# Opening of a fused conditioning, recurrence and FFN kernel: loads and first products in another order

## The reference, cut to what matters

```python
styles = w @ (affine_w * gain).T + affine_b            # (2, 512), w is 2 x 256
dcoefs = rsqrt(sum((weight * styles)**2, axis=2) + 1e-08)
xm = x * styles[:, None, :]
y = einsum('blc,oc->blo', xm, weight) * dcoefs          # 512 x 512 weight
y = clip(y + bias, -256, 256)

h = rms_norm(y) * norm_w
hs = h @ fc_w.T + fc_b                                  # then fc_r, fc_i, fc_gate:
r, i = sigmoid(h @ fc_r_w.T + ...), sigmoid(h @ fc_i_w.T + ...)
# a gated recurrence over the tokens, an MLP of 1536 columns, then
# a second branch with an int8 product
```

## Time and profile before

| what | value |
|---|---|
| median of the runs | 1724.21 us |
| profiled execution | 1724.23 us |
| its span, first to last instruction | 1722.2 us |
| TensorE busy | 1711.0 us, 99% of the span |
| VectorE, ScalarE, GpSimd busy | 1249.2, 882.0, 728.7 us |

### The profile page before, as it was taken

The page is one execution under the profiler, slowest core; times in us unless marked ns, Lnnn a source line. Parts: engine busy times, 40 slices in busy tenths (PEclk is TensorE's granted clock), DMA queues, the critical chain, the costliest instruction groups (busy, mean ns, idle before and its releaser), DMA issues. The chain is left out here.

```text
span 1722.2 us, 23029 instructions
## 1 busy us (share of the span) xinstructions
PE 1711.0 (99%) x7749; PEld 1385.2 (80%) x7749; DVE 1249.2 (73%) x1842; ACT 882.0 (51%) x1306; POOL 728.7 (42%) x642
## 2 busy tenths in 40 slices
PE   9999999999999999999999999999999999999998
PEld 7888888888888888888888888778787787787776
DVE  7766776658989688687464434447998988888876
ACT  7655556556666576575553222233554444543533
POOL 1122221222677465656571000006656755855823
PEclk9999999999999999999999999999999999999999
DMA  6011101120233434232445666887635444535411
GB/s 211 1 49 50 49 0 49 49 74 25 98 123 105 164 99 147 86 120 89 171 147 191 205 213 212 318 297 257 223 116 156 114 139 146 152 104 163 137 43 61
DMA packets 119959, 221.94 MB, mean 129 GB/s; under 512 B 25442, under 2 KB 25890, under 8 KB 119860
## 3 DMA queue, kind: packets, MB, share of 16 engines
q1 hardware_dynamic: 94308, 161.99, 28.1%
q10 hardware_dynamic: 18384, 33.56, 6.1%
q0 software_dynamic: 7168, 25.17, 4.9%
HBM read 158.26 MB, written 58.75 MB: 126 GB/s over the span
## 5 line engine op out<-in xcount | busy, mean ns | idle before, releaser
L1082 PE MATMUL bank<-h_parts,mlp_w 128*128 128x512 f32 x2016 | 459.2, 389 | 0.6 <-ACT product_copy L1302 0.5
L1082 PEld LDWEIGHTS bank<-h_parts,mlp_w 128*128 128x128 f32 x2016 | 378.1, 188 | 80.4 <-ACT product_copy L1302 1.4
L359 PE MATMUL bank<-h_parts,gate_w 128*128 128x512 f32 x1536 | 351.1, 389 | 0.6 <-DVE h_parts L696 0.6
L359 PEld LDWEIGHTS bank<-h_parts,gate_w 128*128 128x128 f32 x1536 | 288.1, 188 | 61.9 <-issue 0.9
L2161 PE MATMUL bank<-operand_parts,int_w 128*128 128x512 f32 x1152 | 274.9, 394 | 0.1
L1147 PE MATMUL bank<-p_parts,mlp_out_w 128*128 128x512 f32 x1152 | 267.4, 391 | 0.0
L2161 PEld LDWEIGHTS bank<-operand_parts,int_w 128*128 128x128 f32 x1152 | 213.7, 188 | 49.4 <-issue 4.8
L1147 PEld LDWEIGHTS bank<-p_parts,mlp_out_w 128*128 128x128 f32 x1152 | 214.6, 188 | 48.0 <-issue 3.4
L1423 POOL TENSOR_TENSOR product_out<-product_out,gelu 128x512 f32<-128x512 f32 x69 | 119.7, 1755 | 95.9 <-DVE product_out L1582 95.4
L621 POOL TENSOR_TENSOR decay_sq<-decay 128x512 f32<-128x512 f32 x32 | 39.2, 1226 | 278.8 <-DVE decay L709 278.8
L1302 ACT ACTIVATE product_copy<-bank,vec_sb 128x512 f32<-128x512 f32 x144 | 99.0, 687 | 106.3 <-PE bank L1082 105.5
(11 more groups left out here) (322 smaller groups left out, 2733.5 us busy)
## 6 DMA issues: line engine op xcount, KB each, us to landing
p_tile<-p_d ACTq DMA_DIRECT2D x96, 256.0 KB, 4.9
p_d<-product_out SPq DMA_DIRECT2D x92, 256.0 KB, 2.0
raw_mlp_w<-mlp_gate_g SPq DMA_DIRECT2D x21, 512.0 KB, 3.7
raw_mlp_w<-mlp_fc_g SPq DMA_DIRECT2D x21, 512.0 KB, 4.1
xin<-xT SPq DMA_DIRECT2D x8, 1024.0 KB
hs_d<-u SPq DMA_DIRECT2D x8, 1024.0 KB, 5.0
hs_pair<-hs_d SPq DMA_DIRECT2D x8, 1024.0 KB, 7.6
x_columns<-xT SPq DMA_DIRECT2D x8, 1024.0 KB, 6.9
```

The lines of the kernel that those rows point to most:

```text
L359: i = pe.matmul(bank[:], gw[:, w, s, k, m * P:(m + 1) * P], hr[:, q, t, k, :], start=k == 0 and n == 0, stop=k == KT - 1 and n == 2)
L1082: i = pe.matmul(bank[:], wb[g % 2][:, s, w, kk, :], hop[u % 2][o][:, t, kk, :], start=first and kk == 0 and n == 0, stop=kk == 1 and n == ...
```

## The change: what it does

1. `affT`, `cond_wT` and the first input block are now issued from ScalarE's queue, in this order. The input block comes in two halves of 512 KB (tiles 0 and 1, tiles 2 and 3), of which the first has a semaphore of its own, `x_half`. SyncE issues `fc_wT` and `fc_r_wT` once `cond_wT` and that first half have landed.
2. ScalarE's `x_early(0)` waits for the styles, then for the first half, and for the second half only before its third tile.
3. TensorE runs 5 matmuls on constants ahead of the style product (16 before), 6 behind it (3 before), then the high products at once. The first half of the demodulation sums stands behind them, then the low products of tile 0, then the second half of the sums, and then the low products of tiles 1 to 3.
4. VectorE makes six low parts of gate weights ahead of line 819 (two before), and two behind it (six before).

```diff
@@ sync, prepare
                 sp.dma_start(vec[:], ins["vec"]).then_inc(s_vec, 16)
                 sp.dma_start(condT, ins["condT"]).then_inc(s_cond, 16)
-                sp.dma_start(aff, ins["affT"].rearrange("(k p) o -> p k o", p=P)).then_inc(s_aff, 16)
                 sp.wait_ge(w_loaded[0], 16)
-                load(0)
+                sp.wait_ge(x_half, 16)
                 load_weights(1)
@@ tensor, prepare
                 pe.wait_ge(s_dch, 3)
-                keep_clock(16)
+                keep_clock(5)
                 pe.wait_ge(s_cond, 16)
                 pe.wait_ge(s_aff, 16)
...
                 i.then_inc(s_sty_ps, 1)
-                keep_clock(3)
+                keep_clock(6)
+                project_first_high()
                 pe.wait_ge(s_wsq, 2)
                 pe.wait_ge(s_dch, 7)
                 pe.wait_ge(s_sty2, 1)
                 demodulation((0, 1))
-                project_first_high()
+                project_first_low(0)
                 demodulation((2, 3))
-                for m in range(KT):
+                for m in range(1, KT):
                     project_first_low(m)
@@ scalar
             def x_early(b):
-                act.wait_ge(x_loaded, 16 * (b + 1))
                 act.wait_ge(s_sty, BATCH)
+                if b == 0:
+                    act.wait_ge(x_half, 16)
                 for k in range(KT):
+                    if k == (0 if b else 2):
+                        act.wait_ge(x_loaded, 16 * (b + 1))
                     act.activation(XP[b][:, 0, k, :], xin[:, k, :], ACT.Copy, scale=sty[:, k, 0:1]).then_inc(x_high, 1)
...
             def prepare():
+                act.dma_start(aff, ins["affT"].rearrange("(k p) o -> p k o", p=P)).then_inc(s_aff, 16)
                 act.dma_start(raw[:, 0], ins[names[0]].rearrange("(k p) o -> p k o", p=P)).then_inc(w_loaded[0], 16)
+                act.dma_start(xin[:, 0:2], xT[:, 0:2, 0:BT]).then_inc(x_half, 16)
+                act.dma_start(xin[:, 2:KT], xT[:, 2:KT, 0:BT]).then_inc(x_loaded, 16)
@@ vector, prepare
                 split_low(0)
                 x_low_early(0)
-                split_low(1, (0, 1))
+                split_low(1)
+                split_low(2, (0, 1))
                 dve.wait_ge(s_dem_ps, 1)
                 dve.tensor_scalar(small[:, 20:28], I[1][:, 0:8], 1e-8, None, ALU.add).then_inc(s_dem_in, 1)
-                split_low(1, (2, 3))
-                split_low(2)
+                split_low(2, (2, 3))
```

More of the change, by code:

```diff
@@ L231, in w_scale @@
             return v("norm_w", k) if n else 1.0
-        x_loaded, x_high, x_low = sem("x_loaded"), sem("x_high"), sem("x_low")
+        x_half, x_loaded, x_high, x_low = sem("x_half_loaded"), sem("x_loaded"), sem("x_high"), sem("x_low")
         y_ps, y_evac, y_clip, y_sq = sem("y_ps"), sem("y_evac"), sem("y_clipped"), sem("y_squared")
```

## The result

The changed kernel took 1726.87 us, the median of 22 runs (1725.64 to 1728.74), against 1724.54 us (1722.79 to 1726.8, 22 runs) for the kernel before beside it. The ratio is 1.0015, 95% interval 1.0009 to 1.0020. I had forecast 1723.9 us and a range of 1721.9 to 1726.2: the time is above the range, and the change makes the kernel slower, by 2.3 us, which is less than the 0.2% that I had set as the bound. Of the 3.0 us between forecast and median, 0.3 are the kernel before itself: I had counted from the median of 3 runs, 1724.21, and that of 22 is 1724.54.

What follows compares the result with a forecast made beforehand. The prediction took the gates' start to be bound by when ScalarE starts block 1's input. Sums 0.3 us later, less a 0.62 us bank wait, gave gates 0.3 us earlier: 1724.23 - 0.3 = 1723.9 us, range 1721.9 to 1726.2.

Steps and rivals of the forecast that it cites:

- What bounds the kernel: First 41 us: the gates' start is set by when ScalarE starts block 1's input (24.26), not by TensorE's products.
- The second chain: From the sums of line 414 through VectorE, GpSimd and ScalarE's tiles of y to block 1's input and the gates, 40.60.
- Part 1: Opening loads: with affT ahead, cond_wT lands at 7.66, 1.3 us later; input halves at 9.0 and 10.35.
- Part 2: Styles and input: squares from 7.72, styles read from 9.87, ScalarE starts at 10.15, high products at 11.0, 1.55 us earlier.
- C: Rival on the conditioning input: condT lands behind cond_wT at 7.7, high products 1.0 us later, time 1724.9; chance 0.08.
- D: Rival on the input: halves land late, ScalarE starts at 11.7 as before, sums at 21.7, time 1725.5; chance 0.07.
- Part 3: TensorE's order: high products at full pace, then first sums and tile 0's low products; sums end at 20.1, 0.3 us later.
- rival B: Clock at 0.50 over the 16 high products after TensorE's idle time: up to 3.1 us, 1725.5 to 1727.0; chance 0.2.
- Part 4: VectorE's six low parts ahead of reading the sums: done at 19.7, 0.4 us before the sums, so no cost.
- The sum: Sums at 20.1, the 0.62 us bank wait goes, block 1's input at 23.95 against 24.26, gates 0.3 us earlier: 1723.9 us.
- A shift of that point shifts the end by the same: Rest of the kernel from the first gate products at 40.60: unchanged, so any shift there moves the end equally.

Runs made afterwards that it cites:

- e5: e4 with the second demodulation sums directly behind the first, and VectorE's order of the kernel before; 1725.95 us, ratio 1.0008 to the kernel before.
- e7_input_late: e1_warm with the first input block in one piece from SyncE's queue, behind its wait for the weights; 1729.75 us (one run).
- e1_warm: The changed kernel with 16 constant matmuls ahead of the style product instead of 5; 1724.69 us, ratio 1.0001 to the kernel before.
- e4: e1_warm with the conditioning weights ahead of the style table in ScalarE's queue; 1724.01 us, ratio 1.0000 to the kernel before.
- e3: The kernel before with only TensorE's and VectorE's new order, loads and constants as before; 1726.67 us, ratio 1.0014 to the kernel before.
- e9: Repeat run of e4 with TensorE's and VectorE's order of the kernel before; 1723.46 us, ratio 0.9997 to the kernel before.

## Why the prediction was wrong

- **What bounds the kernel: right in its place.** The second chain decides, the products' earlier start (11.89 against 12.58) does not. In every profile but one the gates begin 19.9 to 20.0 us behind the reading of the sums with the new order and 20.8 with the old one; the exception is e5 (23.1), where the low products became slow.
- **Part 1, the loads: mis-sized.** Forecast 7.66 for the weights, measured 8.56. Without the input right behind them on the queue they landed at 7.86 (e7_input_late), so the style table ahead costs nearly what I had worked out, and 0.7 went with the input, in one profile. I had let it follow "without a stop" at no price.
- **Part 2: right given that.** Squares (8.59 against my 7.72), styles (10.76 against 9.87) and ScalarE's start (11.03 against 10.15) each lie 0.9 behind, by the late weights. `condT` landed behind `affT` alone, so C did not happen; D neither.
- **Part 3, TensorE's order: right in what it adds, wrong in the clock.** First sums 1.7 us and tile 0's low products 1.9 stand on the path, as forecast. But I put the high products at the full pace, 3.7, and they took 4.6. This is the step that failed most plainly. That was rival B, to which I gave 0.2; e1_warm takes those 0.9 us back. I had even noted that the constants ahead were fewer, and costed the 6 "at the worse pace", without asking what that pace said about the instructions behind them. The style product, which I took at 1.85 from a warm row, took 3.57.
- **Part 4, VectorE: right that it costs nothing.** It was ready at 20.96, 1.3 later than my 19.7, but the sums were 1.9 late, and it waited 1.07 us for them; in e4, with the sums read at 20.42, it still waited 0.57. ScalarE began on `fc_wT` only at 15.53, where I had put 13.1.
- **The sum:** 0.9 (weights) + 0.9 (clock) on -0.3 make 1.5; measured at the gates 1.38.
- **"A shift of that point shifts the end by the same": failed by 1.0 us.** In the medians of the profiles the part behind the gates, untouched by the change, takes 1.0 us more, for the most part by a wait at 1262. Neither the forecast nor a rival had a place for that. The sum of both is 1.9; the 0.4 us up to the 2.3 of the medians stay open, since all seven profiles lie below the median of the 22 runs. Both losses go when the constants and the weights' place are put back (e4_weights_first, 0.1 from the kernel before), though the link from the opening to the far wait is not shown.

## What to carry to other kernels

Work that fills an idle engine is free only where it stands: moved behind the work that it was waiting for, the first sums and tile 0's products cost their full 3.6 us on the chain to the scale. A queue is a resource in both directions: a transfer put ahead of the critical one costs its bytes, and one put right behind it may cost too: 0.4 to 0.7 us for the weights here, nothing for the style table. When constants that keep the clock up are taken away, price everything behind them at the slow pace until a row shows the contrary.

## What the runs showed of the hardware that I had not expected

- Two-column float32 products depend on the clock as well: 16 rows in 1.85 us at the full pace and in 3.57 at the slow one. With 32 such rows in one series the clock fell within the series and stayed at 0.50 for 6.83 us (e5_sums_together), although dense products stood on both sides.
- The same kernel meets the fall of the clock for 3.4 or for 6.8 us from one execution to the next (before: 40.60 and 41.93 at the gates). These 1.3 us are a third of the 4 us between its fastest and slowest run.
- Four VectorE instructions on 20x128 elements (`bias_table`) took a time that went by steps, with how far GpSimd's run of instructions of 1.29 us began behind them: 1.41 us when it began 1.19 to 1.74 us behind their start, 2.35 to 2.45 at 0.77 to 1.02, 3.36 at 0.55 (e3), 4.33 at 0.26 (e9), and 5.19 to 5.39 when it began ahead of them. So each of the four costs 0.35 us alone, and about 1 us more when GpSimd is under way.
- The Trainium skill ("SBUF — State Buffer", Who interferes with whom) states that a VectorE instruction with two inputs in SBUF contends with a GpSimd instruction that reads SBUF, by an exclusive lock, so that the later one waits until the other is through. These rows agree, over all 20 profiles: nought, one, two, three or four of the instructions wait, and each for most of one of GpSimd's. No run here took the port apart from other causes.
